# A log-polar convolution with batch norm: two of the vector engine's column sums built by adding DMA transfers, and the bank additions ahead of the third pair's sums

## The chip, the cores and the metric

The kernel runs on one core of one Trainium2 chip. The metric is the device time of one execution in microseconds. The kernel before takes 1685.85 us (median of 3 runs, 1685.67 to 1686.25).

## What is computed

x is 32 images x 256 channels x 28 x 28, float32. Twelve fixed masks of 9 x 9 (two radius levels by six angles, without the centre pixel) pool each channel; each mask is an average over its bin. A full convolution (256 to 256 channels) takes the 12 pooled planes, a 1 x 1 convolution takes x itself, and the sum goes through batch norm over all images, is added to x and clipped at zero:

```
xp  = log_pooling(x)                                # 12 bins, laid out 4 x 3 per pixel
out = conv(xp, w_conv1, stride=(4, 3)) + conv(x, w_center) + b_center
out = (out - mean(out)) * rsqrt(var(out) + 1e-5)    # mean and var over images, rows, columns
return relu(out * gamma + beta + x)
```

## The kernel before, in words

The 256 channels lie on 128 partitions as two halves, c = 0 and c = 1. Images are stored by columns: a plane is 28 columns of 28 values, and in x_pad each half has two columns of zeros on each side. The program has two phases: a loop over 32 images that computes the convolution output y and writes it to DRAM, and a tail that normalizes, adds x, clips and stores.

In the first phase one step s = 2 * image + c is one half of one image. VectorE (DVE) builds sums of shifted columns and rows out of x_pad:

- `d03` and `inner` hold differences and sums of neighbours (the small ring); their split goes to `inner_split`.
- `row2` holds sums of two neighbouring columns (L526). `row3` (L534) adds a third column to it, `row3v` (L540) adds two rows, `box4` and `box3` (L556, L558) add more rows.
- `ends` holds sums of columns four apart (L536).
- The three "pairs" j = 0, 1, 2 of outer bins are sums of these: j = 0 is box4 + row2 and j = 1 is box3 + row2 (`pooled_sums`, L486), j = 2 is box3 + ends, in two instructions (`short_sum`, L494).

A matrix product in float32 precision is made of three passes over float32r operands: ScalarE (ACT) rounds a tile to its high part (L324, L327, L334), DVE subtracts to get the low part (L403, in `lo_of_pooled` and in the two splits of `inner`), and TensorE (PE) multiplies high by high, low weights by high, and high by low (L625 to L627).

PE runs per step: the middle products into PSUM banks 4 to 7 (36 matmuls of 406 columns), the inner products (24 of 392 columns) into banks 0 to 3, and the three pairs (72 of 364 columns) into banks 0 to 3. Both halves of an image accumulate in the same banks, so an image is 264 matmuls, and y is complete after c = 1. It is then taken from PSUM by DVE: `take_middle` (banks 4 to 7) and `take_y` (banks 0 to 3: the "bank additions", L465), both of the previous image, inside the step c = 0 of the next. PE may start the inner products of an image only when `take_y` of the image before has signalled `y_ready` (L657).

The order on each engine is written out by hand. On SyncE (SP) the queue is: the loads of x for the next image when `x_used` says that DVE has finished with x_pad, and the store of y. GpSimd (POOL) only writes zeros at the start. Of the buffers of the sums there is one each, so a sum of step s + 1 can be written only when the pairs of step s have read it.

After the last image DVE and ACT compute the batch norm's factors (L586 to L606). The tail loads y and x back (SP), DVE scales and adds, ACT clips and stores. Its first loads start as soon as the buffers of phase one come free.

## Time and profile before

| | |
|---|---|
| median of 3 runs | 1685.85 us |
| the profiled execution's own time | 1686.6 us |
| its span | 1684.8 us |
| mean granted TensorE clock over the span | 0.949 of full speed |
| busy: PE, DVE, ACT, POOL | 88%, 91%, 38%, 0% |
| DMA over the span | 129.54 MB, mean 77 GB/s |

How to read it: durations come from one profiled execution, whose span (first to last instruction) is 1.8 us shorter than its own time. The span has three stretches: a start of some 90 us in which DVE also prepares the weights, the even loop over the images up to 1531 us, and the tail of 150 us in which the DMA queues move 380 to 425 GB/s. In the loop both PE and DVE are nearly always busy, so which of them sets the time is not told by the shares.

### The profile page before, as it was taken

How to read it: one execution, taken by the hardware profiler on the slowest of the kernel's cores; microseconds unless marked ns; L12 is line 12 of the kernel's file. 1: busy time of each engine (PE TensorE's matmuls, PEld its weight loads, DVE VectorE, ACT ScalarE, POOL GpSimd, SP SyncE). 2: the span in 40 equal slices, each digit the busy share in tenths (PEclk: the TensorE clock that was granted, in tenths of full speed). 3: DMA queues.
4: the chain of work that ended last, by engine and by line, in shares of the span. 5: the costliest groups of instructions: out<-in, count | busy, mean ns of one | idle time of the engine just before them, and what ended most of it. 6: DMA issues, size and time to landing. Idle time of an engine off the chain costs nothing.

```text
span 1684.8 us, 21919 instructions
## 1 busy us (share of the span) xinstructions
PE 1489.2 (88%) x8468; PEld 1476.5 (88%) x8468; DVE 1531.3 (91%) x1455; ACT 645.3 (38%) x689; POOL 2.7 (0%) x21
## 2 busy tenths in 40 slices
PE   6899999999999999999999999999999999993000
PEld 6899999999999999999999999999999999993000
DVE  8999999999999999999999999999999999995423
ACT  3234343343333434334333343433433334434423
POOL 0000000000000000000000000000000000000000
PEclk8999999999999999999999999999999999997555
DMA  2010111001111011100111101111011110149999
GB/s 110 20 38 29 38 38 38 21 27 38 38 38 38 29 38 38 38 29 19 38 38 38 38 29 38 38 38 37 11 38 38 38 38 29 38 159 421 425 424 382
DMA packets 28615, 129.54 MB, mean 77 GB/s; under 512 B 3520, under 2 KB 3520, under 8 KB 28608
## 3 DMA queue, kind: packets, MB, share of 16 engines
q1 hardware_dynamic: 23744, 103.77, 17.0%
q10 hardware_dynamic: 4864, 25.69, 3.7%
q8 instruction: 2, 0.03, 0.0%
q14 instruction: 5, 0.04, 0.0%
HBM read 78.88 MB, written 50.58 MB: 77 GB/s over the span
## 4 chain that ended last, share of the span: by engine, by line
PE 50%; DVE 27%; issue 11%; SPq 5%; ACT 4%; DMA 3%; DVEq 0%; ACTq 0%
PE acc L625 17%; PE acc L627 16%; PE acc L626 16%; DVE pooled_split L403 6%; DVE pooled L402 6%; DVE inner_split L403 5%; SPq L266 3%; ACT inner_split L324 3%; DVE box L402 2%; DVE y_stage L402 2%; DVE row L402 2%; DMA phase<-x 2%; SPq L263 2%; DMA out<-phase 1%; ACT phase L394 0%
## 5 line engine op out<-in xcount | busy, mean ns | idle before, releaser
L334 ACT ACTIVATE pooled_split<-pooled 128x1456 fp32r<-128x1456 f32 x192 | 273.4, 1425 | 608.0 <-DVE pooled L402 608.0
L403 DVE TENSOR_TENSOR pooled_split<-pooled,pooled_split 128x1456 fp32r<-128x1456 f32 x192 | 317.4, 1667 | 0.3 <-ACT pooled_split L334 0.3
L625 PE MATMUL acc<-inner_split,w_first 128*128 128x406 f32 (+1 forms) x640 | 225.7, 353 | 36.3 <-DVE y_stage L402 25.0
L625 PE MATMUL acc<-pooled_split,w_first 128*128 128x364 f32 x768 | 253.6, 330 | 2.4 <-DVE pooled_split L403 2.4
L625 PE MATMUL acc<-pooled_split,w_outer 128*128 128x364 f32 x768 | 252.3, 329 | 1.1 <-DVE pooled_split L403 1.1
L626 PE MATMUL acc<-pooled_split,w_first 128*128 128x364 f32 x768 | 252.6, 329 | 0.0
L627 PE MATMUL acc<-pooled_split,w_first 128*128 128x364 f32 x768 | 252.5, 329 | 0.0
L626 PE MATMUL acc<-pooled_split,w_outer 128*128 128x364 f32 x768 | 252.2, 328 | 0.0
L627 PE MATMUL acc<-pooled_split,w_outer 128*128 128x364 f32 x768 | 251.8, 328 | 0.0
L627 PE MATMUL acc<-inner_split,w_first 128*128 128x406 f32 (+1 forms) x640 | 222.8, 348 | 0.0
L625 PE MATMUL acc<-inner_split,w_inner 128*128 128x406 f32 (+1 forms) x640 | 221.2, 346 | 1.1 <-DVE inner_split L403 1.1
L626 PE MATMUL acc<-inner_split,w_first 128*128 128x406 f32 (+1 forms) x640 | 222.0, 347 | 0.0
L627 PE MATMUL acc<-inner_split,w_inner 128*128 128x406 f32 (+1 forms) x640 | 221.0, 345 | 0.0
L626 PE MATMUL acc<-inner_split,w_inner 128*128 128x406 f32 (+1 forms) x640 | 220.5, 344 | 0.0
L402 DVE TENSOR_TENSOR pooled<-box,row 128x1456 f32<-128x1456 f32 x128 | 208.1, 1666 | 0.0
L324 ACT ACTIVATE inner_split<-inner 128x1600 fp32r<-128x1600 f32 x64 | 98.7, 1542 | 209.3 <-PE acc L627 200.7
L625 PEld LDWEIGHTS acc<-inner_split,w_first 128*128 128x128 f32 x640 | 121.6, 190 | 47.3 <-DVE y_stage L402 35.4
L403 DVE TENSOR_TENSOR inner_split<-inner,inner_split 128x1600 fp32r<-128x1600 f32 x64 | 116.8, 1824 | 42.2 <-ACT inner_split L324 42.2
L625 PEld LDWEIGHTS acc<-pooled_split,w_first 128*128 128x128 f32 x768 | 144.4, 188 | 2.7 <-DVE pooled_split L403 2.7
L350 ACT ACTIVATE m_copy<-y_stage,minus_pivot 128x784 f32<-128x784 f32 x128 | 121.3, 948 | 64.7 <-DVE y_stage L402 50.1
L625 PEld LDWEIGHTS acc<-pooled_split,w_outer 128*128 128x128 f32 x768 | 144.3, 188 | 1.4 <-DVE pooled_split L403 1.4
L626 PEld LDWEIGHTS acc<-pooled_split,w_first 128*128 128x128 f32 x768 | 144.4, 188 | 0.0
(82 smaller groups left out, 2200.7 us busy)
## 6 DMA issues: line engine op xcount, KB each, us to landing
x_pad<-x SPq DMA_DIRECT2D x64, 392.0 KB, 3.3
y_dram<-y_stage SPq DMA_DIRECT2D x31, 784.0 KB, 5.0
phase<-y_dram SPq DMA_DIRECT2D x30, 784.0 KB, 28.3
phase<-x SPq DMA_DIRECT2D x30, 784.0 KB, 30.5
out<-phase ACTq DMA_DIRECT2D x30, 784.0 KB, 16.0
w_stage<-w_raw SPq DMA_DIRECT2D x2, 896.0 KB, 7.7
out<-x_pad ACTq DMA_DIRECT2D x2, 784.0 KB, 20.4
w_stage<-w_raw SPq DMA_DIRECT2D x2, 768.0 KB, 9.1
```

The costliest lines, as they stand in the source:

```text
L263: sp.dma_start(y_slot(d), y_dram[tail_image(round_, d)]).then_inc(tail_loaded[d], 16)
L266: sp.dma_start(x_slot_whole(d), x[tail_image(round_, d)].rearrange("p c w h -> p c (w h)"))\
L324: nc.scalar.activation(view(inner_split, 0, (1, SD)), view(inner, 0, (1, SD)), ACT.Copy)\
L334: nc.scalar.activation(view(pooled_split, 2 * j * PAIR, (1, PAIR)), view(pooled, (PAIRS * c + j) % 2 * PAIR, (1, PAIR)), ACT.Copy)\
L350: nc.scalar.activation(m1_copy[:, :], view(y_stage, o * HW, (1, HW)), function, bias=minus_pivot[:, o:o + 1], accum_out=sums[:, bass.ds((k ...
L402: add = lambda out_, a, b: nc.vector.tensor_tensor(out_, a, b, ALU.add)
L403: sub = lambda out_, a, b: nc.vector.tensor_tensor(out_, a, b, ALU.subtract)
L625: nc.tensor.matmul(place, hi_w, hi_in, start=start, stop=False)
L626: nc.tensor.matmul(place, lo_w, hi_in, start=False, stop=False)
L627: return nc.tensor.matmul(place, hi_w, lo_in, start=False, stop=stop)
```

## The change

Four things change.

- `row2` and `ends` are no longer computed by DVE. A new input `x_wide` holds x with two columns of zeros at the left and right and four zeros above and below each column (pitch 36). For each step SP copies one shifted part of x_wide into the buffer (`begin_sum`), and when it has landed POOL issues a DMA with `accum_op=ADD` (`add_from`) that adds a second part, shifted by one column (row2) or four (ends). row2 is 128 x 1116 elements, ends 128 x 1008.
- The copy into row2 for step s + 1 waits on `pooled_ready` for the second pair of step s, that into ends for the third pair's sums.
- `take_y` moves ahead of the two `short_sum` instructions (in c = 0); before, it stood behind them and behind the low part of pair 1.
- The loads of x wait on `row3_ready` and not on `x_used`; each is followed on SP by the two copies, and the store of y comes behind those of c = 1. POOL's zeroing of row2 and of the edges of ends goes, since the transfers bring the zeros.

The names d, row and box in the rows of the profile stand for d03, row2 and row3, box3 and box4 (numbers are left out there).

```diff
-        ZEROED = 17
+        ZEROED = 14
...
-                         row2[:, :],
...
-                         view(ends, 0, (ENDS_H, W), (1, 2)), view(ends, H + 2, (ENDS_H, W), (1, 2))):
+                         view(box3, 0, (BOX3_H, W + 2)), view(box3, H + 3, (BOX3_H, W + 2))):
...
+            def add_from(image, c, buf, first_column, n_columns):
+                return pool.dma_start(view(buf, 0, (1, n_columns * TALL_PITCH)),
+                                      x_wide[bass.ds(image, 1), :, c, bass.ds(
+                                          (first_column + EDGE) * TALL_PITCH, n_columns * TALL_PITCH)]
+                                      .rearrange("n p f -> p (n f)"), accum_op=ALU.add)
+
+            def wait_first(semaphore, count):
+
+                pool.wait_ge(semaphore, count)
+                nc.gpsimd.sem_inc(sum_turns, 1)
+
+            def image_sums(image):
+                for c in range(CH):
+                    s = CH * image + c
+                    wait_first(row2_begun, 16 * (s + 1))
+                    add_from(image, c, row2, -1, W + 3).then_inc(row2_ready, 16)
+                    wait_first(ends_begun, 16 * (s + 1))
+                    add_from(image, c, ends, 2, W).then_inc(ends_ready, 16)
+
+            image_sums(0)
+            with pool.Fori(1, IMAGES) as image:
+                image_sums(image)
         @block.sync
         def _(sp):
...
+            def begin_sum(image, c, buf, n_columns, begun):
+                sp.dma_start(view(buf, 0, (1, n_columns * TALL_PITCH)),
+                             x_wide[bass.ds(image, 1), :, c, 0:n_columns * TALL_PITCH]
+                             .rearrange("n p f -> p (n f)")).then_inc(begun, 16)
+
+            def begin_sums(image, c):
+
+                s = CH * image + c
+                wait_from_one(sp, pooled_ready, PAIRS * s - 1)
+                begin_sum(image, c, row2, W + 3, row2_begun)
+                wait_from_one(sp, pooled_ready, PAIRS * s)
+                begin_sum(image, c, ends, W, ends_begun)
+
             def load_weights(c):
                 for part, (first, end) in enumerate(((0, RAW_OUTER), (RAW_OUTER, RAW))):
                     sp.dma_start(view(w_stage, (c * RAW + first) * CHANNELS, (1, (end - first) * CHANNELS)),
                         .then_inc(w_loaded[c][part], 16)
             def image_steps(image, first=False, last=False):
-                if not last:
-                    for c in range(CH):
-                        sp.wait_ge(x_used, CH * image + c + 1)
+                for c in range(CH):
+                    if not last:
+                        sp.wait_ge(row3_ready, CH * image + c + 1)
                         load_x(image + 1, c)
-                if not first:
-                    sp.wait_ge(y_ready, CH * image + FREE)
-                    sp.dma_start(y_dram[bass.ds(image - 1, 1)].rearrange("n p f -> p (n f)"),
-                                 y_stage[:, :]).then_inc(y_saved, 16)
+                    if c == 0:
+                        begin_sums(image, 1)
+                    elif not last:
+                        begin_sums(image + 1, 0)
+                    if c == 0 and not first:
+                        sp.wait_ge(y_ready, CH * image + FREE)
+                        sp.dma_start(y_dram[bass.ds(image - 1, 1)].rearrange("n p f -> p (n f)"),
+                                     y_stage[:, :]).then_inc(y_saved, 16)
...
             load_x(0, 0)
             load_weights(0)
+            begin_sums(0, 0)
             load_x(0, 1)
             load_weights(1)
             for dst, src in ((bias, b_center), (gam, gamma), (bet, beta)):
...
-                           view(ends, 6 * m, (ENDS_H, 2), (2 * ENDS_H, u), (1, h)))
+                           view(ends, RIM - 2 + 6 * m, (ENDS_H, 2), (2 * ENDS_H, u), (1, h)))
...
-                    wait_from_one(dve, pooled_ready, PAIRS * s)
-                    add(view(row2, ROW2_H + 4, (ROW2_H, W + 1), (1, H)), columns(-1, 1, W + 1),
-                        columns(0, 1, W + 1)).then_inc(row2_ready, 1)
-
                     dve.wait_ge(inner_hi_ready, 2 * s + 1)
                     sub(view(inner_split, INNER, (1, SD)), view(inner, 0, (1, SD)),
                         view(inner_split, 0, (1, SD)).bitcast(F32)).then_inc(inner_lo_ready, 1)
-                    dve.wait_ge(row2_ready, s + 1)
+                    dve.wait_ge(row2_ready, 16 * (s + 1))
                     add(view(row3, 1, (ROW3_H, W + 2), (1, H)), view(row2, 4, (ROW2_H, W + 2), (1, H)),
                         columns(0, 1, W + 2)).then_inc(row3_ready, 1)
-                    add(view(ends, 2, (ENDS_H, W), (1, H)), columns(-2, 1, W), columns(2, 1, W))\
-                        .then_inc(ends_ready, 1)
...
-                    dve.wait_ge(ends_ready, s + 1)
-                    nc.vector.sem_inc(x_used, 1)
...
                     lo_of_pooled(s, c, 0)
+                    if c == 0 and not first:
+                        take_y(image - 1)
+                    dve.wait_ge(ends_ready, 16 * (s + 1))
                     short_sum(s, c, 0)
                     short_sum(s, c, 1).then_inc(pooled_ready, 1)
                     lo_of_pooled(s, c, 1)
-                    if c == 0 and not first:
-                        take_y(image - 1)
                     lo_of_pooled(s, c, 2)
...
+    x_cols = np.ascontiguousarray(
+        np.asarray(x).reshape(images, 128, halves, height, width).transpose(0, 1, 2, 4, 3))
+    x_wide = np.pad(x_cols, ((0, 0), (0, 0), (0, 0), (2, 2), (4, 4))).reshape(images, 128, halves, -1)
```

On DVE, in the loop over the images, step c = 0 from the sums of pairs 0 and 1 to the low part of pair 2, before:

```order
L402 TENSOR_TENSOR pooled<-box4,row2 128x1456 [waits pooled_lo_ready]
L402 TENSOR_TENSOR pooled<-box3,row2 128x1456 [waits pooled_lo_ready,box3_ready]
L499 REGISTER_ALU
L403 TENSOR_TENSOR pooled_split<-pooled,pooled_split 128x1456 [waits pooled_hi_ready]
L402 TENSOR_TENSOR pooled<-box3,ends 128x728 [waits pooled_lo_ready] x2
L499 REGISTER_ALU
L403 TENSOR_TENSOR pooled_split<-pooled,pooled_split 128x1456 [waits pooled_hi_ready]
L461 REGISTER_ALU
L402 TENSOR_TENSOR y_stage<-acc,y_stage 128x2x14x28 [waits middle_taken,pooled_done]
L402 TENSOR_TENSOR y_stage<-acc,y_stage 128x2x14x28
```

The same place now:

```order
L448 TENSOR_TENSOR pooled<-box4,row2 128x1456 [waits pooled_lo_ready]
L448 TENSOR_TENSOR pooled<-box3,row2 128x1456 [waits pooled_lo_ready,box3_ready]
L545 REGISTER_ALU
L449 TENSOR_TENSOR pooled_split<-pooled,pooled_split 128x1456 [waits pooled_hi_ready]
L507 REGISTER_ALU
L448 TENSOR_TENSOR y_stage<-acc,y_stage 128x2x14x28 [waits middle_taken,pooled_done]
L448 TENSOR_TENSOR y_stage<-acc,y_stage 128x2x14x28
L448 TENSOR_TENSOR pooled<-box3,ends 128x728 [waits pooled_lo_ready,ends_ready]
L448 TENSOR_TENSOR pooled<-box3,ends 128x728 [waits pooled_lo_ready]
L545 REGISTER_ALU
L449 TENSOR_TENSOR pooled_split<-pooled,pooled_split 128x1456 [waits pooled_hi_ready]
```

The two additions into y_stage moved up past the third pair's two sums and one low part, and the sums have a new wait, ends_ready.

On DVE, the same step, from the two-column sum to the box sums, before:

```order
L402 TENSOR_TENSOR row2<-x_pad 128x29x28 [waits pooled_ready]
L529 REGISTER_ALU
L403 TENSOR_TENSOR inner_split<-inner,inner_split 128x1600 [waits inner_hi_ready]
L402 TENSOR_TENSOR row3<-row2,x_pad 128x30x28 [waits row2_ready]
L402 TENSOR_TENSOR ends<-x_pad 128x28x28
L402 TENSOR_TENSOR row3v<-row3 128x30x29 [waits row3_ready]
L543 REGISTER_ALU
L403 TENSOR_TENSOR inner_split<-d03,inner_split 128x784 [waits inner_hi_ready]
L402 TENSOR_TENSOR box4<-row3v 128x930 [waits ends_ready,row3v_ready]
```

The same place now:

```order
L449 TENSOR_TENSOR inner_split<-inner,inner_split 128x1600 [waits inner_hi_ready]
L575 REGISTER_ALU
L448 TENSOR_TENSOR row3<-row2,x_pad 128x30x28 [waits row2_ready]
L448 TENSOR_TENSOR row3v<-row3 128x30x29 [waits row3_ready]
L583 REGISTER_ALU
L449 TENSOR_TENSOR inner_split<-d03,inner_split 128x784 [waits inner_hi_ready]
L448 TENSOR_TENSOR box4<-row3v 128x930 [waits row3v_ready]
```

Two instructions are gone, and row2_ready, which row3 waits for, is now signalled by a DMA.

On SP, one image of the loop, before:

```order
L239 ISA [waits x_used]
L239 DMA x_pad<-x 128x784
L252 REGISTER_ALU
L239 ISA [waits x_used]
L239 DMA x_pad<-x 128x784
L256 ISA [waits y_ready]
L256 DMA y_dram<-y_stage 128x1568
```

and now (up to the second load of x; the two copies come again behind that one):

```order
L267 ISA [waits row3_ready]
L267 DMA x_pad<-x 128x784
L219 ISA
L272 ISA [waits pooled_ready]
L272 DMA row2<-x_wide 128x1116
L272 DMA ends<-x_wide 128x1008 [waits pooled_ready]
L301 ISA [waits y_ready]
L301 DMA y_dram<-y_stage 128x1568
L293 REGISTER_ALU
```

Four copies per image joined the queue of SP, each behind a wait. On POOL, which had nothing in the loop, one step is now:

```order
L242 ISA [waits row2_begun]
L242 DMA row2<-x_wide 128x1116
L242 ISA [waits ends_begun]
L242 DMA ends<-x_wide 128x1008
L249 ISA
```

The adding transfer of a buffer is queued behind the landing of its copy.

## Rows read from the trace of the kernel before

**Rows 1.** Waits: engine line <- releaser: us in total, times, longest us.

```profile
ACT inner_split L324 <- PE acc L627: 200.7, 60, 3.4
...
DVE inner_split L403 <- ACT inner_split L324: 42.2, 60, 1.1
...
PE acc L625 <- DVE y_stage L402: 25.0, 31, 8.6
```

**Rows 2.** Windows, one image: stretch us, busy us (instructions) per engine, PEclk, DMA, GB/s.

```profile
701.88:713.89 12.01, 12.01 (x74) 12.01 (x73) 10.96 (x10) 5.27 (x7) 0.00 (x0) 1.00 0.30 100
713.89:724.89 11.00, 11.00 (x62) 10.99 (x61) 10.97 (x12) 4.11 (x4) 0.00 (x0) 1.00 0.00 0
724.89:736.83 11.94, 11.94 (x74) 11.94 (x74) 11.60 (x11) 3.23 (x3) 0.00 (x0) 1.00 0.11 34
736.83:748.60 11.77, 11.24 (x62) 10.90 (x61) 11.74 (x13) 5.42 (x7) 0.00 (x0) 1.00 0.00 0
```

**Rows 3.** Timeline of PE, end of one image: start us, us, instruction [idle before].

```profile
743.34 0.34 PE L627 MATMUL acc<-inner_split,w_first 128*128 128x406 f32 x1
744.21 0.44 PE L625 MATMUL acc<-inner_split,w_first 128*128 128x392 f32 x1 [0.53 <-DVE y_stage L402]
744.50 0.34 PE L626 MATMUL acc<-inner_split,w_first 128*128 128x392 f32 x1
```

**Rows 4.** Timeline of DVE, the same image, from the pairs of the step before.

```profile
711.19 3.25 DVE L402 TENSOR_TENSOR pooled<-box,row 128x1456 f32<-128x1456 f32 x2
...
725.38 0.99 DVE L402 TENSOR_TENSOR row<-x_pad 128x812 f32<-128x812 f32 x1
726.72 1.83 DVE L403 TENSOR_TENSOR inner_split<-inner,inner_split 128x1600 fp32r<-128x1600 f32 x1 [0.34 <-ACT inner_split L324]
728.46 1.03 DVE L402 TENSOR_TENSOR row<-row,x_pad 128x840 f32<-128x840 f32 x1
729.40 0.97 DVE L402 TENSOR_TENSOR ends<-x_pad 128x784 f32<-128x784 f32 x1
...
734.20 3.25 DVE L402 TENSOR_TENSOR pooled<-box,row 128x1456 f32<-128x1456 f32 x2
737.37 1.67 DVE L403 TENSOR_TENSOR pooled_split<-pooled,pooled_split 128x1456 fp32r<-128x1456 f32 x1
739.07 1.74 DVE L402 TENSOR_TENSOR pooled<-box,ends 128x728 f32<-128x728 f32 x2
...
742.31 1.84 DVE L402 TENSOR_TENSOR y_stage<-acc,y_stage 128x784 f32<-128x784 f32 x2
```

**Rows 5.** The page, part 6: DMA issues, KB each, median us to landing.

```profile
x_pad<-x SPq DMA_DIRECT2D x64, 392.0 KB, 3.3
y_dram<-y_stage SPq DMA_DIRECT2D x31, 784.0 KB, 5.0
...
w_stage<-w_raw SPq DMA_DIRECT2D x2, 768.0 KB, 9.1
```

**Rows 6.** Timelines of DVE and PE in the first two images.

```profile
18.54 1.02 DVE L402 TENSOR_TENSOR row<-row,x_pad 128x840 f32<-128x840 f32 x1
...
55.19 3.24 DVE L402 TENSOR_TENSOR pooled<-box,row 128x1456 f32<-128x1456 f32 x2
...
72.14 1.02 DVE L402 TENSOR_TENSOR row<-row,x_pad 128x840 f32<-128x840 f32 x1
...
81.05 1.67 DVE L403 TENSOR_TENSOR pooled_split<-pooled,pooled_split 128x1456 fp32r<-128x1456 f32 x1
...
85.99 1.85 DVE L402 TENSOR_TENSOR y_stage<-acc,y_stage 128x784 f32<-128x784 f32 x2
...
87.89 0.69 PE L625 MATMUL acc<-inner_split,w_first 128*128 128x392 f32 x1 [8.58 <-DVE y_stage L402]
```

**Rows 7.** Windows: the 5 us behind the first wait for y.

```profile
88.00:93.00 5.00, 5.00 (x19) 5.00 (x20) 4.79 (x9) 0.44 (x1) 0.00 (x0) 0.61 0.00 0
```

**Rows 8.** Windows: the last 23 us of the loop over the images.

```profile
1508.00:1531.00 23.00, 23.00 (x135) 22.97 (x133) 9.08 (x8) 4.27 (x4) 0.00 (x0) 1.00 0.96 389
```

More of the change, by code:

```diff
@@ L5, with conv_bn_relu_program @@
 from concourse import mybir
-def conv_bn_relu_program(nc, x, w_raw, b_center, gamma, beta, out, y_dram):
+def conv_bn_relu_program(nc, x, x_wide, w_raw, b_center, gamma, beta, out, y_dram):
     F32 = mybir.dt.float32
@@ L16, in conv_bn_relu_program @@
     IMAGES, P, CH, W, H = x.shape
+    EDGE, RIM = 2, 4
+    TALL_PITCH = H + 2 * RIM
     CHANNELS = P * CH
@@ L53, in conv_bn_relu_program @@
     PAIR = 4 * HALF_PLANE
-    ROW2_H, ROW3_H, ROW3V_H, BOX4_H, BOX3_H, ENDS_H = H + 8, H + 3, H + 5, H + 3, H + 4, H + 4
+    ROW3_H, ROW3V_H, BOX4_H, BOX3_H = H + 3, H + 5, H + 3, H + 4
+    ROW2_H = ENDS_H = TALL_PITCH
     X_PAD = (W + 4) * H
@@ L169, in conv_bn_relu_program @@
         x_loaded = [sem(f"x_loaded{c}") for c in range(CH)]
-        x_used = sem("x_used")
         d_ready = sem("d_ready")
@@ L174, in conv_bn_relu_program @@
         inner_lo_ready = sem("inner_lo_ready")
+        row2_begun = sem("row2_begun")
         row2_ready = sem("row2_ready")
+        ends_begun = sem("ends_begun")
+        sum_turns = sem("sum_turns")
         row3_ready = sem("row3_ready")
@@ L224, in _ @@
                          view(inner, 0, (MIDDLE, 2), (PITCH, U + 1)), view(inner, MIDDLE - 1, (MIDDLE, 2)),
-                         row2[:, :],
                          view(row3, 0, (ROW3_H, W + 2)), view(row3, H + 1, (ROW3_H, W + 2), (1, 2)),
                          view(row3v, 0, (ROW3V_H, W + 2), (1, 2)), view(row3v, H + 3, (ROW3V_H, W + 2), (1, 2)),
-                         view(box3, 0, (BOX3_H, W + 2)), view(box3, H + 3, (BOX3_H, W + 2)),
-                         view(ends, 0, (ENDS_H, W), (1, 2)), view(ends, H + 2, (ENDS_H, W), (1, 2))):
+                         view(box3, 0, (BOX3_H, W + 2)), view(box3, H + 3, (BOX3_H, W + 2))):
                 if edge.dtype == F32R:
@@ L699, in per_partition @@
         return np.ascontiguousarray(np.asarray(v).reshape(128, -1))
+    x_cols = np.ascontiguousarray(
+        np.asarray(x).reshape(images, 128, halves, height, width).transpose(0, 1, 2, 4, 3))
+    x_wide = np.pad(x_cols, ((0, 0), (0, 0), (0, 0), (2, 2), (4, 4))).reshape(images, 128, halves, -1)
     arrays = {
-        "x": np.ascontiguousarray(
-            np.asarray(x).reshape(images, 128, halves, height, width).transpose(0, 1, 2, 4, 3)),
+        "x": x_cols,
+        "x_wide": x_wide,
         "w_raw": w_raw,
```

## The prediction

> **What bounds the kernel now.** The busy shares of the page come first, PE 88% and DVE 91% in the table above: they don't tell which of the two sets the pace. The waits do [rows 1]. In the loop ACT waits for PE before it splits `inner` (200.7 us in all), and DVE waits for ACT there (42.2 us): DVE is held back by PE once per step, so DVE is not the engine that sets the pace alone. PE waits for one thing in the loop: for DVE's bank additions into y_stage, 31 times, 25.0 us, the longest 8.6. The windows [rows 2] take one image apart: 12.01 + 11.00 + 11.94 + 11.77 = 46.72 us, with PE busy in every microsecond of the first three. The fourth holds the wait. The timeline of PE [rows 3] shows its size: 36 middle matmuls from 736.83 stand (743.34 - 736.83) / 35 = 0.186 apart, so the inner products could start at 743.53. They start at 744.21, 0.68 later, and the second of them follows after 0.29 instead of (748.60 - 744.50) / 23 = 0.178, another 0.11 of refilling. An image therefore has 45.93 us of PE work and 0.79 us of stall. PE is the floor and the bank additions are all that stands above it. The timeline of DVE [rows 4] says why they are late: PE finished the image by about 737.0, but the two additions start at 742.31, because DVE was at the low part of pair 0 (from 737.37), the third pair's sums (739.07) and another low part. So in the even loop the change can win 0.79 us per image and no more, whatever it takes off DVE.
>
> **The move of the bank additions, and the work taken off DVE.** The sum of columns four apart costs DVE 0.89 us of its time (from 729.40, 0.97 long, with 0.08 of it under the next one, as 728.46 to 729.40 holds a 1.03 us instruction) [rows 4]. Without it row3v follows row3 directly and must wait for its end instead of starting 0.09 before it, so I count 0.78 with a little for the hand-over. The two-column sum (0.99 long, 0.91 by the same reckoning) stood in front of the split of `inner`; in the even loop DVE waits there anyway for ACT (0.34 idle), and the chain behind it hangs on PE through ACT, so this one wins nothing there. The low part of pair 0 then ends at 737.37 + 1.67 - 0.78 = 738.3. The bank additions come next: 738.3 to 740.1. PE wants them at 743.53, so they are 3.4 us early and the stall of 0.79 goes whole. It was 31 times less the first: 30 x 0.79 = 23.7 us. What is late next: the low part of pair 1, now about 740.1 + 1.7 + 1.6 = 743.4, against its use by PE at 743.53 + 4.3 + 4.0 = 751.8; nothing. The third pair's sums move 1.1 us later in such a step (739.07 - 0.78 + 1.84 = 740.1), and behind them ACT's split and two low parts follow one another as they do in the steps c = 1. The other queues: the store of y comes behind the copies into ends on SP, and these wait for the third pair's sums, which end at 741.9, 2 us before the old additions' end (744.15); y_stage is next written in the following image, so the store has its time. SP's loads of x start a little earlier than now (behind row3 and not behind ends).
>
> **The start.** Up to the first bank additions DVE alone sets the time: PE's first wait for y ends at 87.89 after 8.58 us [rows 6]. There every DVE instruction counts. Three steps lie before it. Each loses 0.91 + 0.78 = 1.7 us, together 5.1; the low part of pair 0 moves from 81.05 to 75.95 and ends at 77.6. The additions then run at 77.6 to 79.5 instead of 85.99 to 87.8: 8.4 us earlier. PE has its middle products done by then (before: 87.89 - 8.58 = 79.3, and the chain of DVE that released them is 3.4 us shorter, so 75.9). PE still waits 3.6 us instead of 8.6.
>
> **The clock behind that wait.** In the 5 us behind the wait the granted clock is 0.61, a mix of the two levels 1.2 and 2.4 GHz [rows 7], after 8.58 us without a matmul. What it costs: from 87.89 to the same place 14 images later, 744.21, are 656.3 us, and 14 x 46.72 = 654.1, so 2.2 us. With 3.6 us of waiting it may fall again (0 won) or not (2.2 won). I take the middle, 1.1.
>
> **What replaces the two sums: copies and adding transfers.** Four copies per image on SP and four adding transfers on POOL, 2 x (558 + 504) KB each way, a load on the queues of some 4.3 MB per 46 us, 95 GB/s beside the 34 to 38 of now; the queues carry 389 in the last 23 us of the loop [rows 8]. Their volume is no limit. Their latency may be. A load of 392 KB lands in 3.3 us, a store of 784 KB in 5.0 [rows 5]: 1.6 + 1.7 per 392 KB, so the copy into row2 (558 KB) takes 4.0, with SP's issue 4.3. No row shows an adding transfer or one issued by POOL. Bounds for T, from POOL's wake-up to landing: below, 3.3 us, as the 392 KB load; above, 13.2 us, the slowest kind outside the tail (9.1 us for the 768 KB of weights, queued behind others [rows 5]) with the bytes twice: 9.1 x 2 x 558 / 768. An addition must read what stands in the buffer as well as the new data, so I count its bytes twice: 1.6 + 2 x 2.4 = 6.4, and take that, since the plain loads and stores of the loop are the nearest rows.
>
> The trace has no such row, but the Trainium skill, "Collectives: The Full Stack", Part 3, under "Why ReduceScatter is half of AllGather", says that an add in the DMA engine costs nothing itself and only doubles the reads. By its factor the transfer takes the same 6.4; no run here shows it yet. "DMA: Bandwidth & Descriptors" ("Anatomy of one DMA") gives 2.0 us + bytes / 436e3 for a transfer issued there; an estimate by that page, with the bytes twice, is 4.6.
>
> **The time there is for row2.** The pairs that read it end at 711.19 + 3.25 = 714.4, now 713.7, and row3 wants it at 728.46 [rows 4]: 14.8 us for 4.3 + T, so T up to 10.5. Seen as a loop: from row3 to the end of the second pair are 737.4 - 728.46 = 9.0, now 8.2 us; a step lasts 8.2 + 4.3 + T when the transfers set it, against 22.96 of PE. Below T = 10.4 PE sets the pace, at 10.8 the loop is as slow as before. With 6.4 there are 4 us of room, of which the ends copy and the store of y, on the same queues, can take perhaps 2. ends has some 20 us for itself. Behind a late row2 on DVE stand row3 and everything to the pairs, and for those ACT and PE wait. At the start, where DVE sets the pace, the margins are smaller. The third step's row2 is free at 55.19 + 3.24 = 58.4, now 55.0, would land 10.7 later at 65.7, and is wanted at 72.14, now 4.3 earlier at 67.8 [rows 6]. The first one's copy is queued behind the second part of the first weights, which takes 9.1 us from its issue [rows 5] at 1.6 or so: landed at 10.7 at the earliest, with T at 17.1, and wanted at 18.54, now 17.6 [rows 6]. I count nothing for either, and up to 5 us at the other end.
>
> **The tail.** It begins with loads that wait for buffers which PE and DVE free at the end of the loop, and in the last 23 us of it the queues are already at 0.96 [rows 8]. The bytes of the tail are the same and their gates move with PE's end, so it keeps its length. Only the last ends transfers, 1 MB or so, may lie in it: up to 2 us.
>
> **The sum.** 1686.6 (the profiled execution's own time) - 8.4 - 1.1 - 23.7 = 1653.4. The median of the runs is 0.75 lower than that execution, so about 1652.7; I write 1653.
>
> **The rivals.**
> - *The adding transfers are slow.* T over 10.8 us, in both steps of an image, and row3 waits for row2. Each image takes 2 x (12.5 + T): at T = 12 49.0 us, 2.3 more than now over 31 images, 1685.85 + 71 = 1757; at the upper bound of 13.2, 51.4, so 1831. For it: no row shows such a transfer, 558 KB in 12 us would be only 48 GB/s, and the store of y shares the queues. Against it: 784 KB land in 5.0. It decides from T = 10.8.
> - *They are in time in the loop but not at the start.* T between 8.5 and 10.4, or the first row2 late behind the weights: up to 5 us at the first step and 2 at the second and third lost of the 8.4, 1656 to 1664. Nothing speaks for it but the thin margins.
> - *The stall stays, only the start wins*: the wait of PE is taken over by another (row2 late by over 3.4 us in the steps c = 0 only, from the store of y and ends on the queues): 1686 - 9.5 = 1676 or, with more, no change.
> - *All the work off DVE counts*: 31 x 2 x 1.7 = 105 us less. PE's 45.93 us of work per image exclude it.
>
> **Chances.** The forecast 0.65 (own range 1649 to 1658), the late start 0.08, the stall that stays 0.05, slow transfers 0.20, and 0.02 for other things that leave the time as it is. Within 0.2%, some 3.4 us, is what a measurement of this kernel can hardly tell from no change. Faster 0.76, same 0.04, slower 0.20. The range 1647 to 1690 leaves out the slow transfers and little else.
>
> **What would show it.** Right: PE's waits for y_stage fall from 31 to one of 3 to 4 us at 76 to 80 us; an image takes 45.9 us; DVE's busy time falls by 64 x (0.99 + 0.97) = 125 us and its wait for ACT grows; row3 waits for nothing, or for the DMA of row2 a few times at the start; an adding transfer lands in 5 to 8 us. Wrong: row3 waiting for row2's DMA in every step, with an image of over 46.72 us; then the term T was mis-sized. If PE still waits in front of the inner products with the DMA in time, the step on the order of DVE's work was wrong.

## The result, and the profile after

| | before | after |
|---|---|---|
| median, us | 1685.98 (1685.67 to 1686.25, 4 runs) | 1657.08 (1656.24 to 1657.47, 4 runs) |
| ratio | | 0.9828 [0.9811, 0.9845] |
| profiled execution: span, own time, us | 1684.8, 1686.6 | 1655.8, 1657.47 |
| last matmul of the loop begins, us | 1530.95 | 1501.96 |
| one image in the loop, us | 46.72 | 45.96 |

29 us faster, against 33 forecast, inside the range of 1647 to 1690. The 29 us are there when the loop ends (1530.95 - 1501.96), and the span is shorter by the same 29.0, so the tail kept its length.

The page of the changed kernel, its shares (part 1) and its DMA issues (part 6: KB each, median us to landing):

```profile
PE 1483.6 (90%) x8468; PEld 1481.7 (89%) x8468; DVE 1419.4 (86%) x1327; ACT 641.7 (39%) x689; POOL 112.5 (7%) x146
...
row<-x_wide SPq DMA_DIRECT2D x64, 558.0 KB, 3.7
row<-x_wide POOLq DMA_DIRECT2D x64, 558.0 KB, 7.3
ends<-x_wide SPq DMA_DIRECT2D x64, 504.0 KB, 3.9
ends<-x_wide POOLq DMA_DIRECT2D x64, 504.0 KB, 5.8
x_pad<-x SPq DMA_DIRECT2D x64, 392.0 KB, 3.1
y_dram<-y_stage SPq DMA_DIRECT2D x31, 784.0 KB, 8.7
```

The adding transfer of row2, which had no row before, takes 7.3 us where the plain copy of the same bytes takes 3.7. These are medians over both steps of an image: in the steps c = 0 of the loop the adding transfer takes 5.8 to 7.0 us, in the steps c = 1, where the store of y is on the queues too, 7.2 to 8.9. The store went from 5.0 [rows 5] to 8.7 beside these transfers.

The queues of the same page (part 3: packets, MB, share of 16 engines); q0 carries the adding transfers alone, q1 what SP issues:

```profile
q1 hardware_dynamic: 42176, 173.38, 31.1%
q0 software_dynamic: 18432, 69.61, 24.3%
```

Per byte the adding packets hold the DMA engines 1.95 times as long (24.3 / 69.61 against 31.1 / 173.38). By size, from the packet records between 400 and 1300 us, the median packet of row2 (4464 bytes) takes 356 ns when it adds and 173 when it copies.

Waits of the changed kernel (engine line <- releaser: us in total, times, longest us):

```profile
DVE inner_split L449 <- ACT inner_split L370: 119.4, 60, 2.1
...
PE acc L664 <- DVE y_stage L448: 3.4, 1, 3.4
DVE row L448 <- DMA row<-x_wide: 2.4, 1, 2.4
```

Read against [rows 1]: PE's wait for y fell from 31 times and 25.0 us to once and 3.4. DVE's busy time fell by 112 us (1531.3 to 1419.4; the 125 of the forecast count the ends of the instructions that overlap twice), while its waits for ACT grew by 77 (42.2 to 119.4): DVE was not the floor. row3 waits for row2's DMA once.

One image of the changed kernel in windows (stretch us, busy us of PE, PEld, DVE, ACT, POOL, PEclk, DMA, GB/s), against [rows 2]:

```profile
700.00:711.30 11.30, 11.30 (x65) 11.30 (x64) 9.36 (x11) 4.43 (x4) 1.76 (x2) 1.00 0.78 172
711.30:722.60 11.30, 11.30 (x69) 11.30 (x68) 11.27 (x10) 2.97 (x3) 0.00 (x0) 1.00 0.18 44
722.60:734.20 11.60, 11.60 (x67) 11.59 (x66) 9.51 (x11) 5.51 (x7) 1.73 (x2) 1.00 0.74 205
734.20:745.96 11.76, 11.76 (x71) 11.76 (x70) 11.62 (x10) 5.00 (x7) 0.00 (x0) 1.00 0.41 100
```

PE is busy in all 45.96 us. The same stretch of DVE (start us, us, instruction, [idle before]), against [rows 4]:

```profile
710.70 1.83 DVE L449 TENSOR_TENSOR inner_split<-inner,inner_split 128x1600 fp32r<-128x1600 f32 x1 [1.94 <-ACT inner_split L370]
712.44 1.03 DVE L448 TENSOR_TENSOR row<-row,x_pad 128x840 f32<-128x840 f32 x1
713.50 1.06 DVE L448 TENSOR_TENSOR row3v<-row 128x870 f32<-128x870 f32 x1
...
720.59 1.67 DVE L449 TENSOR_TENSOR pooled_split<-pooled,pooled_split 128x1456 fp32r<-128x1456 f32 x1
722.17 1.85 DVE L448 TENSOR_TENSOR y_stage<-acc,y_stage 128x784 f32<-128x784 f32 x2
723.94 1.73 DVE L448 TENSOR_TENSOR pooled<-box,ends 128x728 f32<-128x728 f32 x2
```

The additions start 11.47 us behind the split of `inner`; before it was 742.31 - 726.72 = 15.59 [rows 4]. Of the 4.1 us between, 0.8 is the sum of columns four apart and 3.3 the order.

The start, DVE and then PE, against [rows 6]:

```profile
19.34 1.03 DVE L448 TENSOR_TENSOR row<-row,x_pad 128x840 f32<-128x840 f32 x1 [2.39 <-DMA row<-x_wide]
...
77.89 1.67 DVE L449 TENSOR_TENSOR pooled_split<-pooled,pooled_split 128x1456 fp32r<-128x1456 f32 x1
79.47 1.85 DVE L448 TENSOR_TENSOR y_stage<-acc,y_stage 128x784 f32<-128x784 f32 x2
```

```profile
81.38 0.70 PE L664 MATMUL acc<-inner_split,w_first 128*128 128x392 f32 x1 [3.36 <-DVE y_stage L448]
```

PE resumes at 81.38 instead of 87.89: 6.5 us earlier, where 8.4 were forecast. The windows behind that wait, against [rows 7]:

```profile
81.40:86.40 5.00, 5.00 (x15) 5.00 (x16) 5.00 (x5) 1.42 (x1) 0.86 (x1) 0.50 0.53 79
86.40:91.40 5.00, 5.00 (x29) 5.00 (x29) 4.79 (x11) 1.99 (x4) 0.82 (x1) 0.92 0.94 299
```

A granted clock of 0.50 throughout is the lower level, 1.2 GHz; 0.92 is 0.8 us of it in 5. So 5.8 us at the lower level, against (1 - 0.61) x 2 x 5 = 3.9 before [rows 7], though the wait was 3.36 us and not 8.58.

**Where the 29.0 us are.** PE resumes 6.51 earlier. From there to the first matmul of image 2 (the third; they count from 0) it takes 41.95 (81.38 to 123.33) instead of 41.12 (87.89 to 129.01): -0.83, about what the windows give for the clock. Image 2 takes 45.96 instead of 47.14 (PE waited 0.95 for y in it): 1.18. From there to the last matmul 1332.67 instead of 1354.80: 22.13. Sum 28.99.

### The profile page after: what moved, and what is told of

Its sections match the earlier page's. It is cut to its first block, busy times and chain, and to the rows that moved or that the text cites. A ratio compares the mean times of both kernels' runs of the same rounds, so it can differ in the third digit from the quotient of the medians.

```text
span 1655.8 us, 22787 instructions
## 1 busy us (share of the span) xinstructions
PE 1483.6 (90%) x8468; PEld 1481.7 (89%) x8468; DVE 1419.4 (86%) x1327; ACT 641.7 (39%) x689; POOL 112.5 (7%) x146
## 3 DMA queue, kind: packets, MB, share of 16 engines
q1 hardware_dynamic: 42176, 173.38, 31.1%
q0 software_dynamic: 18432, 69.61, 24.3%
## 4 chain that ended last, share of the span: by engine, by line
PE 86%; SPq 5%; DMA 4%; DVE 3%; ACT 1%; issue 1%; ACTq 0%; DVEq 0%; POOLq 0%
PE acc L664 29%; PE acc L665 29%; PE acc L666 29%; SPq L311 3%; DMA phase<-x 2%; SPq L308 2%; DMA row<-x_wide 1%; DMA out<-phase 1%; DVE pooled L448 1%; ACT phase L440 0%; DVE pooled_split L449 0%; DVE inner_split L449 0%; ACT m_copy L396 0%; DVE y_stage L448 0%; DVE row3v L448 0%
## 5 line engine op out<-in xcount | busy, mean ns | idle before, releaser
L449 DVE TENSOR_TENSOR inner_split<-inner,inner_split 128x1600 fp32r<-128x1600 f32 x64 | 116.8, 1825 | 119.4 <-ACT inner_split L370 119.4
L664 PEld LDWEIGHTS acc<-pooled_split,w_first 128*128 128x128 f32 x768 | 144.9, 189 | 4.2 <-DVE pooled_split L449 4.2
L666 PEld LDWEIGHTS acc<-pooled_split,w_first 128*128 128x128 f32 x768 | 144.9, 189 | 0.0
L665 PEld LDWEIGHTS acc<-pooled_split,w_first 128*128 128x128 f32 x768 | 144.9, 189 | 0.0
L666 PEld LDWEIGHTS acc<-pooled_split,w_outer 128*128 128x128 f32 x768 | 144.4, 188 | 0.0
L665 PEld LDWEIGHTS acc<-pooled_split,w_outer 128*128 128x128 f32 x768 | 144.4, 188 | 0.0
```

What stands on the lines that cost most here:

```text
L449: sub = lambda out_, a, b: nc.vector.tensor_tensor(out_, a, b, ALU.subtract)
L664: nc.tensor.matmul(place, hi_w, hi_in, start=start, stop=False)
L665: nc.tensor.matmul(place, lo_w, hi_in, start=False, stop=False)
L666: return nc.tensor.matmul(place, hi_w, lo_in, start=False, stop=stop)
```

## Experiments

**e1_move_only: the order alone.** The kernel before, with only this moved:

```diff
                     lo_of_pooled(s, c, 0)
+                    if c == 0 and not first:
+                        take_y(image - 1)
                     short_sum(s, c, 0)
                     short_sum(s, c, 1).then_inc(pooled_ready, 1)
                     lo_of_pooled(s, c, 1)
-                    if c == 0 and not first:
-                        take_y(image - 1)
```

> The kernel before with one edit: take_y stands ahead of the two short sums. No transfer is added. Theory (the stall needs only 0.8 us of the 3.4 us by which the change brought the additions forward): the low part of pair 0 ends at 739.0, the additions run to 740.9, PE wants them at 743.53, so the whole loop stall of 0.79 us per image goes; DVE has 45.26 us of work in 45.95. At the start the additions come 3.3 us earlier (82.7 to 84.6), PE's first wait falls from 8.6 to 5.3 us, its clock cost stays 2 to 3 us. 1686 - 23.3 - 3.3 = 1659 to 1660, within 3 us of the changed kernel. Rival (once the stall is gone DVE, with 45.26 us of work and its waits for ACT of 1.4 per image, sets the pace): 46.4 us or more per image, 1686 - 10 - 3 = 1673. Second rival (the transfers do the work): 1680 or more.

1659.32 us (1658.67 to 1660.88, 5 runs), ratio 0.9842 [0.9829, 0.9856]. Its waits:

```profile
DVE inner_split L403 <- ACT inner_split L324: 21.5, 31, 0.7
...
PE acc L625 <- DVE y_stage L402: 6.3, 2, 5.2
```

and PE's timeline:

```profile
83.98 0.70 PE L625 MATMUL acc<-inner_split,w_first 128*128 128x392 f32 x1 [5.23 <-DVE y_stage L402]
```

The loop's stall is gone with no transfer at all: 45.92 us per image from image 3 on (image 2 takes 47.25 and still waits 1.06 for y). PE resumes 3.9 us earlier than before, 3.35 of it between the low part of pair 0 and the additions, the 3.3 forecast for the order; the other 0.56 is DVE's earlier beginning in this execution (6.59 against 7.16, when the first weights landed). The move of two lines brings 27 of the 29 us.

**e2_sums_only: the transfers alone.** The changed kernel with `take_y` back in its old place, the same lines the other way round.

> The changed kernel with take_y at its old place, behind the low part of pair 1. The transfers stay. Theory: taking the sum of columns four apart off DVE brings the low part of pair 0 forward by 0.78 us, so the additions end at about 743.4 in the clock of the image before, 0.1 us before PE wants them; the loop stall shrinks from 0.79 to 0 to 0.2 us, 18 to 23 us won. At the start the additions come 6.5 - 3.3 = 3.2 us earlier than before. 1660 to 1665. Rival (the order is what counts, the sums taken off DVE hide behind its wait for ACT): the stall stays at 0.5 us or more, 1672 to 1680.

1663.23 us (1662.84 to 1663.6, 4 runs), ratio 0.9863 [0.9848, 0.9878]. PE's waits:

```profile
PEld acc L664 <- DVE y_stage L448: 11.2, 31, 5.9
...
PE acc L664 <- DVE y_stage L448: 5.6, 1, 5.6
```

Again one wait of PE for y instead of 31, and 46.05 us per image: 0.8 us off DVE is just enough for a stall of 0.8. It leaves no room: the weight load (PEld) still waits for y in every image, some 0.2 us, and 0.09 us per image are left of the stall. So each part alone takes the loop's stall, with 27 and 23 us in all, and together they bring 29: the two overlap in the loop, and their gains add only at the start.

**e3_first_row2: is the first row2 late because its copy is queued late?** The copy is issued between the two parts of the first weights and no longer behind both:

```diff
-            def load_weights(c):
+            def load_weights(c, begin_row2=False):
...
+                    if begin_row2 and part == 0:
+                        begin_sum(0, 0, row2, W + 3, row2_begun)
...
-            load_weights(0)
-            begin_sums(0, 0)
+            load_weights(0, begin_row2=True)
...
+            begin_sum(0, 0, ends, W, ends_begun)
```

> The changed kernel with SP's first queue in another order: the copy into row2 of step 0 goes between the two parts of the first weights, the copy into ends behind all the weights. Theory (row3 of step 0 waited 2.4 us for row2's adding transfer, which shared the queues with the copy into ends and the weights): the adding transfer lands 2 to 3 us earlier, row3's wait falls from 2.4 to 0 to 0.5 us, the first bank additions come 2 to 2.4 us earlier and PE waits 1 us for them instead of 3.4. That alone is 1655; if the clock then does not fall, another 2.7 is won, 1652. Rival (the weights' second part, now behind the copy, is late for ACT and DVE, or the queue is the limit and the transfer lands no earlier): 1657 to 1659.

1655.92 us (1655.37 to 1656.42, 5 runs), ratio 0.982 [0.9807, 0.9833]. DVE's timeline:

```profile
18.82 1.03 DVE L450 TENSOR_TENSOR row<-row,x_pad 128x840 f32<-128x840 f32 x1 [1.57 <-DMA row<-x_wide]
```

The adding transfer was issued 1.7 us earlier (POOL's row at 8.60 instead of 10.31) and landed 0.5 earlier, where 2 to 3 were expected; it took 10.2 us there, beside the weights, against 9.0 in the changed kernel. The window from its issue to its landing shows why:

```profile
8.60:18.80 10.20, 1.42 (x4) 1.41 (x5) 8.61 (x12) 6.41 (x9) 1.00 (x1) 0.56 1.00 323
```

The DMA engines are busy all the time (share 1.00). So the place in the queue counts for 0.5, and the rest is most likely the bytes that the first 19 us must bring; no run took bytes away there while keeping the transfer. The median is 1.2 us below the changed kernel's. In the profiled executions the two resume 0.5 apart, and 1.1 more is a shorter stretch at the lower clock (40.88 us from the resuming to image 2, against 41.95).

**e7_first_on_dve: without the transfer that is late.** Step 0 makes its two-column sum on DVE, as before the change, and POOL sets all of row2 to zero first:

```diff
+                    if first and c == 0:
+                        add(view(row2, ROW2_H + 4, (ROW2_H, W + 1), (1, H)), columns(-1, 1, W + 1),
+                            columns(0, 1, W + 1)).then_inc(row2_first, 1)
...
-                    dve.wait_ge(row2_ready, 16 * (s + 1))
+                    if first and c == 0:
+                        dve.wait_ge(row2_first, 1)
+                    else:
+                        dve.wait_ge(row2_ready, 16 * s)
```

> The changed kernel with row2 of step 0 alone computed on DVE as in the kernel before (0.91 us); POOL zeroes all of row2 again. All other steps take the transfers. Theory: row3 of step 0 starts at 17.9 instead of 19.3, everything on DVE up to the first bank additions is 1.4 us earlier, PE's first wait for y falls from 3.4 to 2.0; 1657.1 - 1.4 = 1655.6. If the clock does not fall behind the shorter wait, 2.7 less: 1653. Rival (the weights arrive later or earlier by as much from run to run): no difference beyond 0.7 us.

1656.35 us (1654.76 to 1656.56, 5 runs), ratio 0.9823 [0.981, 0.9837]. DVE's timeline, and PE's:

```profile
17.86 1.02 DVE L452 TENSOR_TENSOR row<-row,x_pad 128x840 f32<-128x840 f32 x1
```

```profile
79.90 0.45 PE L675 MATMUL acc<-inner_split,w_first 128*128 128x392 f32 x1 [3.85 <-DVE y_stage L452]
```

row3 of step 0 starts 1.48 us earlier and PE resumes 1.48 earlier: what the late transfer cost comes back on PE one for one, also through the wait for y. The profiled own times differ by 2.7, of which 1.1 is the clock (from the resuming to the first matmul of image 2 40.89, against 41.95). The medians differ by 0.7 only, half of the 1.5, and the runs of the two kernels overlap; so the 1.5 us are shown on the profiled executions' rows and not by the times, where the rival (no difference beyond 0.7) is not excluded.

**e6_keep_warm: does work in the wait hold the clock?** The first two images' PE program is written out, and 20 matmuls of 104 columns into a bank's unused end stand ahead of the inner products that wait (the 20 start-up matmuls write up to that end too, which the excerpt leaves out):

```diff
+                    if c == 0:
+                        for _ in range(keep_warm):
+                            nc.tensor.matmul(view(acc, 8 * BANK - 104, (1, 104)), view(w_first, 0, (1, P)),
+                                             view(w_first, 0, (1, 104)), start=False, stop=False)
...
+            image_steps(0)
+            image_steps(1, keep_warm=WARM_AGAIN)
```

> The changed kernel with the images 0 and 1 of PE written out ahead of the loop, and in image 1, between the middle products and the wait for y, 20 matmuls of 104 columns into columns that nothing reads. They fill some 2 of the 3.4 us that PE waits there. Theory (what the clock costs behind that wait, 2.7 us, comes from PE's idling): the granted clock behind the wait stays at 2.4 GHz, 1657 - 2.7 = 1654.4. Rival (short matmuls, or the rest of the wait, don't keep it, or the clock falls for what PE did before): 1657, or 1658 if the matmuls outlast the wait.

1655.77 us (1654.96 to 1656.71, 5 runs), ratio 0.982 [0.9807, 0.9833]. PE's timeline:

```profile
77.76 2.33 PE L695 MATMUL acc<-w_first 128*128 128x104 f32 x20
81.54 0.42 PE L665 MATMUL acc<-inner_split,w_first 128*128 128x392 f32 x1 [1.45 <-DVE y_stage L449]
```

The wait without a matmul is 1.45 us and the clock falls all the same, half a microsecond behind the resuming; from there to the first matmul of image 2 are 40.87 us, hardly less than e3's 40.88 behind an idle wait of 3.52. So the extra matmuls did not hold the clock. The profiled execution is 1.0 us shorter than the changed kernel's: 1.1 by the shorter stretch at the lower level, as in e3 and e7, with PE resuming 0.2 later. What makes up the 1.3 us between the medians is not shown.

That 1.45 us without a matmul are enough for a fall is not shown by this. e7's trace has a wait of 1.48 us behind ordinary matmuls, and the clock stays up:

```profile
33.09 0.44 PE L675 MATMUL acc<-pooled_split,w_first 128*128 128x364 f32 x1 [1.48 <-DVE pooled_split L453]
```

```profile
33.10:38.10 5.00, 5.00 (x30) 5.00 (x31) 4.96 (x5) 1.43 (x1) 0.87 (x1) 1.00 0.60 177
```

So the 20 short matmuls seem not to stand for ordinary ones, the rival that the expectation names; between ordinary matmuls e6 has 3.8 us (77.76 to 81.54). No run with ordinary matmuls in that wait decides it.

**e4_add_twice: what do slow transfers cost?** The adding transfer of row2 is issued twice, one behind the other (row2 then holds one column too often):

```diff
+                    add_from(image, c, row2, -1, W + 3).then_inc(row2_half, 16)
+                    wait_first(row2_half, 16 * (s + 1))
                     add_from(image, c, row2, -1, W + 3).then_inc(row2_ready, 16)
```

> The changed kernel with row2's adding transfer issued twice for every step, the second when the first has landed, and row3 waiting for the second; row2 is then not the sum that is wanted. It tests the point from which the transfers would set the pace. Theory: a step lasts, when the transfers set it, from row3 to the copy's issue 8.4 us, from there to POOL's issue 4.4 to 5.1, and then T; T doubles from 7.3 to 14.6 plus some 0.5 for the second issue: 28.3 us per step, 56.6 per image against 45.96, 1657 + 31 x 10.6 = 1986. If the second transfer runs alone on the queues in 5.5 us, 52.6 per image, 1865. Rival (lateness of row2 is absorbed by what DVE and PE have buffered): 1657 to 1700.

1878.02 us (1876.69 to 1879.35, 2 runs), ratio 1.1138 [1.1118, 1.1158]. Its waits:

```profile
DVE row L451 <- DMA row<-x_wide: 292.2, 64, 9.1
...
PE acc L667 <- DVE y_stage L451: 143.6, 31, 7.0
```

and its DMA issues:

```profile
row<-x_wide POOLq DMA_DIRECT2D x128, 558.0 KB, 6.0
```

row3 now waits in every one of the 64 steps, and the wait for y is back 31 times: an image of the loop takes 49.2 to 54.7 us, in the mean the 52.6 of the branch in which the second adding transfer alone takes 5.5; it took 5.8. The rival of slow transfers is real as a mechanism; only its condition was not met.

**e5_small_add: how near is it?** The second adding transfer brings one column of zeros, so row2 keeps its value and only the time grows:

```diff
-                    add_from(image, c, row2, -1, W + 3).then_inc(row2_ready, 16)
+                    add_from(image, c, row2, -1, W + 3).then_inc(row2_half, 16)
+                    wait_first(row2_half, 16 * (s + 1))
+                    add_from(image, c, row2, -1, 1).then_inc(row2_ready, 16)
```

> The changed kernel with a second, small adding transfer behind row2's (one column, 36 elements per partition), for which row3 waits; the first column of row2 is then not the one that is wanted. It tests how much room there is. Theory: by the trace a step of the transfers lasts 8.4 + 4.4 to 5.1 + 7.3 = 20.1 to 20.8 us against 22.98 of PE, 2.2 to 2.9 us of room. The small transfer costs 2 to 3 us with its issue: row3 waits 0 to 0.5 us in the steps with the shorter room, and 1657 to 1665 comes out. Rival (there is no room beyond what shows, contention grows with it): 46.5 us or more per image, 1675 or more.

1668.45 us (1665.24 to 1675.95, 4 runs), ratio 0.9889 [0.9874, 0.9904]. DMA issues, and waits:

```profile
row<-x_wide POOLq DMA_DIRECT2D x64, 558.0 KB, 7.4
...
row<-x_wide POOLq DMA_DIRECT2D x64, 18.0 KB, 2.4
```

```profile
DVE row L451 <- DMA row<-x_wide: 86.1, 63, 5.3
...
PE acc L667 <- DVE y_stage L451: 11.3, 10, 5.5
```

The small transfer takes 2.4 us and its issue stands 0.6 behind the landing of the first: 3.0 us more per step, and the loop stands on the edge. Of the 29 images from image 2 on 18 take 45.96 to 45.99 us and 11 take 46.2 to 47.4, and the times scatter over 10 us, above the 1657 to 1665 that my theory gave. row3 waits in 63 steps, 1.4 us in the mean, where waits of up to 0.5 in some steps were expected; most of it does not reach PE, which waits for y 10 times. The profile is that of the slowest execution (1675.95). The changed kernel's room is therefore about as long, some 3 us per step in the mean, within the forecast's 4, of which the copy into ends and the store of y were to take perhaps 2.

**e8_first_on_dve_warm: e7 and e6 together** (17 matmuls), the best version that the others point to.

> The same with 17 matmuls of 104 columns between the middle products of image 1 and its wait for y, which take 2.0 us (20 took 2.33), so that PE hardly idles there. Theory: the clock stays high behind them or falls for a shorter time than with 1.45 us of idling left (there 10 slow matmuls, 1.5 us lost): 1652.8 to 1654.5. Rival (short matmuls don't count as work for the clock): it falls as before, 1655.6.

1654.94 us (1653.76 to 1655.12, 5 runs), ratio 0.9813 [0.98, 0.9827]: 2.1 us below the changed kernel. It lies between the theory (1652.8 to 1654.5) and the rival in which the clock falls as before (1655.6). PE idles more than was expected: behind the 17 matmuls it still waits 2.08 us, and the clock falls. e7's profile takes 40.89 us from the resuming to image 2 and this one 40.85, so nothing shows that the extra matmuls have a share in it; the part that a row shows is the 1.5 us of the first row2 (PE resumes at 79.99 instead of 81.38).

## Why the prediction was right, and what missed

**The loop, 23.7 forecast, 23.3 measured (1.18 + 22.13).** The mechanism held: the additions come in time, PE waits for nothing, and the rest of DVE's relief turns into waiting for ACT. An image takes 45.96 where 45.93 was worked out; e1, without transfers, takes 45.92.

What it does not say is which part of the change brings this. It subtracted both parts from DVE's path, came out 3.4 us early, and so had more than the 0.79 us needed, twice over: the order is worth 3.3 and the sum 0.8, and either is enough (the sum all but 0.09 us per image). e1 and e2 show it. The transfers bring only the last 2 us (1659.3 to 1657.1), for a room in the loop that e5 shows to be small.

**The start, 8.4 forecast, 6.5 measured.** The step that failed is "I count nothing for either" on the first row2. The rival of the late start was right in its first half: row3 of step 0 waited 2.39 us. DVE had begun 0.8 us earlier in this execution, since the first weights landed that much sooner, so row3 stands 0.8 later than before (19.34 against 18.54) where the forecast had it 0.9 earlier. That is the whole shortfall of 1.9 within 0.2: the low part of pair 0 is 3.16 earlier instead of 5.1, and the order then gives its 3.3. Steps 1 and 2 gave their 1.7 us each. The working was there (17.1 against 17.6, half a microsecond of room with T at 6.4) and needed only T's real size beside the weights to fall on the other side: POOL issued it at 10.31, sooner than the 10.7 of the forecast, and it took 9.0. The measured 1657.1 lies in the forecast's own range (1649 to 1658) by 1 us, and in the late start's (1656 to 1664) too: at the start it is the rival that describes the run, with a chance of 0.08, and only the loop, the larger term, carried the number.

**The clock, +1.1 forecast, -0.8 measured.** The forecast took the middle between a fall at the old price and none. Its price of 2.2 holds 0.4 that is not the clock: image 2 took 47.14 and not 46.72, for a longer wait for y (won with the loop, in the 1.18). The fall came again, and its cost does not follow the wait's length in these traces. It began 1.0 us before PE resumed in the changed kernel, at the resuming in e1 and 0.5 to 1.4 behind it in e3, e6, e7 and e8. Windows behind the wait in e1 (5.23 us of waiting) and e3 (3.52):

```profile
84.00:89.00 5.00, 5.00 (x19) 5.00 (x20) 5.00 (x5) 1.42 (x1) 0.00 (x0) 0.66 0.00 0
```

```profile
80.90:85.90 5.00, 5.00 (x19) 5.00 (x20) 5.00 (x5) 1.42 (x1) 0.86 (x1) 0.66 0.46 90
```

0.66 over 5 us is 3.4 us at the lower level, a loss of 1.7; before lost 2.0 behind 8.58 us, and the changed kernel's profiled execution 2.9 behind 3.36. The stretches differ from one profiled kernel to the next by as much as the term itself, each seen in one execution; 0 with about 1 us either way would have been the better entry.

The three misses, 0.4 + 1.9 + 1.9, make up the 4.2 us between 33.2 and 29.0.

**T, 6.4 forecast, 7.3 measured.** That the bytes of an addition count twice is borne out by the packets (1.95 times the engines' time per byte). The quotient 7.3 / 3.7 = 2.0 does not show it, since it mixes in what runs beside the transfer: the 504 KB of ends give 5.8 / 3.9 = 1.5, and the second transfers of e4, with less beside them, take 5.8 in the mean, 1.6 times the plain copy. All adding transfers are issued by POOL and all plain ones by SP, so what is the issuing queue's share is not shown. For the packets the trace agrees with the rule of the Trainium skill, "Collectives: The Full Stack", Part 3, "Why ReduceScatter is half of AllGather". The other one, 2.0 us + bytes / 436e3 ("DMA: Bandwidth & Descriptors", "Anatomy of one DMA"), is too low in this kernel also with the bytes doubled: 4.6 as an estimate by that page against 5.8 in e4 and 7.3 here.

"Their volume is no limit" held for the mean and not for the moment. Behind the second copies of an image the engines are full:

```profile
729.00:736.00 7.00, 7.00 (x43) 7.00 (x41) 4.91 (x6) 4.02 (x7) 0.87 (x1) 1.00 1.06 272
```

The share is 1.06 (a packet counts where it begins) at 272 GB/s, while before the change a share of 1.04 stood beside 422 (710 to 712): bytes that are added count once in the GB/s and hold the engines twice as long. In this stretch the store of y and the adding transfer of the step c = 1 are under way (issued at 726.23 and 725.27, 8.7 us each to landing), and that they hold each other up there is the likely reading; no run leaves the store out.

The room: row2's loop per step is now, in the image of the windows above, 8.4 (row3 to the copy's issue) + 4.4 (to POOL's issue) + 8.7 = 21.5 us for c = 1 and 8.4 + 5.1 + 5.8 = 19.3 for c = 0, against 45.96 / 2 = 22.98. Over the loop row2 lands 1.3 to 3.0 us before row3 begins in the steps c = 1 and 3.2 to 4.2 in the others, in the mean about the 3.0 that e5 adds. The 20% for slow transfers were not wasted caution: with 2 x 6.0 (the page's median) e4 shows a kernel at 1878, above the 1757 worked out for T = 12. From the first issue to the second landing are 12.7 us in the mean for c = 0 and 14.5 for c = 1, and with these the branch's own sum, 12.5 + T for each step, gives 52.2 us per image against 52.6. POOL's rows of e4 show part of what comes on top of 12:

```profile
784.10 0.86 POOL L243 DMA_DIRECT2D row<-x_wide  x1 [16.74 <-DMA row<-x_wide]
792.33 0.86 POOL L243 DMA_DIRECT2D row<-x_wide  x1 [7.37 <-DMA ends<-x_wide]
```

The second issue stands 0.6 us behind the landing of the first transfer (791.71), and that one took 7.6 us beside the copy into ends and the store of y. The profile names the copy into ends, which landed 0.2 later, as what ended the wait, but in POOL's program that wait comes behind this issue.

**The tail, constant.** Exact to 0.1 us.

## What to carry to other kernels

Before pricing a change of several parts, ask for each part whether it alone already takes the stall: a stall of 0.8 us can be won only once, and here two moved lines brought nearly all that 256 more transfers brought as well. A sum moved to adding DMA transfers cost here the copy, a hand-over between two queues and an addition whose packets take twice as long; compare that chain with the step, under what else the queues carry at that moment, not the bytes with the mean bandwidth. Entries of half a microsecond at a kernel's start, where every queue is full, deserve a price instead of a zero.

## What the runs showed of the hardware

- Packets that add into SBUF held the DMA engines twice as long as packets that copy: 356 against 173 ns for 4464 bytes, 1.95 times per byte on the page. From issue to landing 558 KB took 5.8 us in the second transfers of e4, 7.3 in the loop (median; the plain copy 3.7), 9.0 and, in e3, 10.2 beside the first weights; 504 KB took 5.8 (plain 3.9), 18 KB 2.4. Adding transfers came from POOL and plain ones from SP, so the two are not separated in these times.
- POOL is busy for 0.86 to 1.1 us to issue one (some 110 us for 128 of them).
- The store of y went from 5.0 to 8.7 us where the DMA engines' share was 1.06 at only 272 GB/s: with additions on the queues a rate well below 400 GB/s was no sign of room.
- TensorE's granted clock fell to its lower level at the waits of 2.65 (e3, image 0), 3.36, 3.52, 3.85, 5.23 and 8.58 us, in the last five for 3.4 to 5.8 us of the work behind them, and not at those of 1.06 and 2.38 (before), 1.48 (e7) and 2.58 us (e1). It fell too at 1.45 us behind 20 matmuls of 104 columns (e6) and at 2.08 behind 17 (e8), so these did not prevent it.
